# A recurrent LSTM kernel: sigmoid for the output gate, a constant scale of h, and h of the second group in smaller pieces

## What is computed

```
xW = einsum('ntd,dg->ntg', x, Wx) + b
def step(carry, xw_t):
    prev_h, prev_c = carry
    a = xw_t + prev_h @ Wh
    i = sigmoid(a[:, :H]); f = sigmoid(a[:, H:2*H]); o = sigmoid(a[:, 2*H:3*H])
    g = tanh(a[:, 3*H:])
    next_c = f * prev_c + i * g
    next_h = o * tanh(next_c)
    return ((next_h, next_c), next_h)
c0 = zeros_like(h0)
hs = scan(step, (h0, c0), xW by time)
out = x + hs
```

## Time and profile before

| what | value |
|---|---|
| median of 3 runs | 1855.11 us (1855.08 to 1855.83) |
| the profiled execution | 1856.47 us |
| its span, first to last instruction | 1854.4 us |
| granted TensorE clock | 1.000 of full speed |
| busy: PE, DVE, ACT, POOL | 90%, 92%, 55%, 29% |

### The profile page before, as it was taken

How to read it: one execution, slowest core, us unless ns; L and a number is a source line. 1 busy time by engine, 2 the same in 40 slices (tenths; PEclk the granted TensorE clock), 3 DMA queues, 4 the chain that set the end, 5 groups by cost and what they waited for, 6 DMA issues and landing times.

```text
span 1854.4 us, 106048 instructions
## 1 busy us (share of the span) xinstructions
PE 1674.3 (90%) x45116; PEld 1065.3 (57%) x45116; DVE 1713.2 (92%) x9739; ACT 1011.4 (55%) x3985; POOL 539.3 (29%) x1560
## 2 busy tenths in 40 slices
PE   1999999999999999999999999999999999999997
PEld 0555555555555555555555555555555555555555
DVE  8999999999999999999999999999999999999998
ACT  4555555555555555555555555555555555555554
POOL 0222223322332222233223332222232233322222
PEclk9999999999999999999999999999999999999999
DMA  5000000000000000000000000000000000000000
GB/s 210 15 26 21 21 23 23 21 21 26 21 21 26 21 21 21 26 21 21 26 21 21 26 21 21 21 27 21 21 26 21 21 24 24 21 21 27 18 12 14
DMA packets 39067, 49.03 MB, mean 26 GB/s; under 512 B 4416, under 2 KB 36160, under 8 KB 38592
## 3 DMA queue, kind: packets, MB, share of 16 engines
q1 hardware_dynamic: 37152, 37.77, 6.3%
q10 hardware_dynamic: 1440, 4.49, 0.6%
HBM read 25.46 MB, written 16.78 MB: 23 GB/s over the span
## 4 chain that ended last, share of the span: by engine, by line
DVE 70%; PE 19%; ACT 7%; issue 3%; DMA 1%; ACTq 0%; DVEq 0%
DVE turned L510 22%; DVE mailbox L514 13%; PE acc L311 12%; DVE products L523 11%; ACT gates L260 7%; PE acc L317 7%; DVE h_halves L538 5%; DVE h_halves L547 3%; DVE gates L532 3%; DVE x_halves L493 3%; DVE out_ring L575 3%; DVE h_feat L542 3%; DVE x_tops L586 2%; DVE mailbox L528 2%; DMA wh<-in_wh 1%
## 5 line engine op out<-in xcount | busy, mean ns | idle before, releaser
L311 PE MATMUL acc<-wh_low,h_halves 128*32 128x256 f16 x16384 | 719.4, 274 | 135.6 <-DVE h_halves L538 133.8
L317 PE MATMUL acc<-wh_high,h_halves 128*32 128x256 f16 x16384 | 722.3, 275 | 0.0
L303 PE MATMUL x_acc<-wx_high,x_halves 128*32 128x512 f16 x8192 | 621.5, 380 | 1.1 <-ACT x_acc L234 1.1
L311 PEld LDWEIGHTS acc<-wh_low,h_halves 128*32 128x32 f16 x16384 | 390.5, 96 | 395.3 <-DVE h_halves L538 383.8
L260 ACT ACTIVATE gates<-mailbox 128x96 f32<-128x96 f32 x1024 | 257.1, 251 | 634.1 <-DVE mailbox L514 634.1
L510 DVE STREAM_TRANSPOSE turned<-acc 128x256 f32<-128x256 f32 x1024 | 458.9, 448 | 57.2 <-PE acc L317 51.4
L194 POOL TENSOR_SCALAR o_gate<-gates,scales 128x32 f32<-128x32 f32 x1024 | 372.7, 364 | 419.4 <-ACT gates L265 419.4
L186 POOL TENSOR_TENSOR o_preact<-turned 128x32 f32<-128x32 f32 x512 | 163.4, 319 | 892.0 <-DVE turned L510 892.0
L317 PEld LDWEIGHTS acc<-wh_high,h_halves 128*32 128x32 f16 x16384 | 343.6, 96 | 113.8
L303 PE MATMUL x_acc<-wx_low,x_halves 128*32 128x512 f16 x4096 | 399.2, 380 | 0.0
L237 ACT ACTIVATE acc<-x_acc,step_mask 128x512 f32<-128x512 f32 x512 | 334.8, 654 | 4.7 <-PE x_acc L303 4.7
(11 more groups left out here) (67 smaller groups left out, 696.5 us busy)
## 6 DMA issues: line engine op xcount, KB each, us to landing
out<-out_ring SPq DMA_DIRECT2D x128, 128.0 KB, 2.1
x_ring<-in_x SPq DMA_DIRECT2D x120, 128.0 KB, 2.9
wx<-in_wx ACTq DMA_DIRECT2D x4, 512.0 KB, 8.1
wx<-in_wx SPq DMA_DIRECT2D x4, 512.0 KB, 8.1
wh<-in_wh SPq DMA_DIRECT2D x4, 512.0 KB, 16.7
wh<-in_wh ACTq DMA_DIRECT2D x4, 512.0 KB, 17.1
x_ring<-in_x SPq DMA_DIRECT2D x2, 512.0 KB, 16.7
b_rows<-in_b ACTq DMA_DIRECT2D x1, 256.0 KB, 21.4
```

The lines of the kernel that those rows point to most:

```text
L303: last = pe.matmul(x_acc[pair % 2][32 * j:32 * j + 32], x_halves[:, pair % (CHUNK // 2), c, half], w[:, c].rearrange("p (n q) g -> p q n g ...
L311: pe.matmul(acc[par][32 * j:32 * j + 32, n, 0:GL], h_halves[1 - par][:, c, 0:2], w_low["wh"][:, c, n * Q + j], start=False, stop=False, sk ...
L317: last = pe.matmul(acc[par][32 * j:32 * j + 32, n, 0:GL], h_halves[1 - par][:, c, 1:3], w_high["wh"][:, c, n * Q + j], start=False, stop=c ...
```

## The change

The output gate becomes ACT's Sigmoid in place of a tanh and a later (t + 1) / 2, and the scale of h is the constant 2^13 in place of one that follows x. The scale of x is now taken out of the masks by which ACT copies `x_acc` into `acc` (`masks`). So POOL's second instruction (L194) goes, and with it `o_gate`; POOL now adds the output gate's halves of both groups, and DVE's `add_last` goes. `high_of_h` and `full_h` become scalar_tensor_tensor instructions with the constant 2^13, and the output row has the constant 2^-13 in place of a `[128, 1]` operand. In group 1, `full_h` and `low_of_h` are each two instructions on one block (16 elements per partition) in place of one on two blocks; `keep_cell(1)` moves behind them. TensorE waits for the low half of block 2 and of block 3 apart. The wait for the kept cells moves from the end of a step to a place behind `turn(0)` of the next. In the setup, ACT runs a Sigmoid on one element first of all, and DVE makes the scales and inverses with some more small instructions.

The diff, cut to its core. Left out are the declarations of the new tiles, the semaphore counts of the scale steps, and the places where `masks` and `step_inverse` take the place of `inverses`.

```diff
@@ -182,17 +187,10 @@
                 pool.wait_ge(out_free[half], 1)
 
             for t in range(T):
-                pool.wait_ge(turned_ready, NG * t + 1)
-                pool.tensor_tensor(o_preact[0][:], turned[0][:, 6:8, 0, :], turned[0][:, 6:8, 1, :], ALU.add)\
-                    .then_inc(o_preact_ready[0], 1)
-                par = t % 2
-                following = (t + 1) // CHUNK % 2
-                if t + 1 < T and (t + 1) % CHUNK == 0 or t == 0:
-                    pool.wait_ge(x_scale_ready, (t + 1) // CHUNK + 1)
                 for n in range(NG):
-                    pool.wait_ge(o_ready, NG * t + n + 1)
-                    pool.tensor_scalar(o_gate[n][:], gates[par][n][:, 4, :], 1.0, scales[following][:, 1:2], ALU.add, ALU.mult)\
-                        .then_inc(h_parts_ready[n], 1)
+                    pool.wait_ge(turned_ready, NG * t + n + 1)
+                    pool.tensor_tensor(o_preact[n][:], turned[n][:, 6:8, 0, :], turned[n][:, 6:8, 1, :], ALU.add)\
+                        .then_inc(o_preact_ready[n], 1)
 
         @block.scalar
         def _(act):
...
@@ -208,6 +206,8 @@
                 act.activation(w_high[k][:, c, :, 64:GL], w32[k][:, c, :, 64:GL], ACT.Copy, scale=half_scale[:, n:n + 1])\
                     .then_inc(done, 1)
 
+            act.wait_ge(ones_ready, 2)
+            act.activation(one_gate[:], ones[:, 0:1], ACT.Sigmoid)
             act.wait_ge(wx_scale_ready, 1)
             for c in range(C):
                 high_of_w("wx", 0, c, wx_high_done)
...
@@ -227,14 +228,17 @@
             high_of_x(0, 1)
             high_of_w("wh", 1, 2, wh_high_done)
             high_of_w("wh", 1, 3, wh_high_done)
-            act.reg_load(rescale[0], inverses[0][0:1, 3:4])
-            act.reg_load(b_scale[0], scales[0][0:1, 3:4].bitcast(I32))
+            for k in range(2):
+                act.reg_load(first_rescale[k], first_inverse[0:1, k:k + 1].bitcast(I32))
+                act.reg_load(rescale[k], step_inverse[0:1, k:k + 1].bitcast(I32))
+            act.reg_load(b_scale[0], scales[0][0:1, 1:2].bitcast(I32))
 
             def place_bias(pair):
                 act.activation(x_acc[pair % 2][:], b_rows[:], ACT.Copy, scale=b_scale[2 * pair // CHUNK % 2]).then_inc(bias_placed, 1)
 
             def fill(t):
-                act.activation(acc[t % 2][:, :, 0:GL], x_acc[t // 2 % 2][:], ACT.Copy, scale=step_mask[:, t % 2:t % 2 + 1])\
+                mask = masks[t // CHUNK % 2] if t > 0 else step_mask
+                act.activation(acc[t % 2][:, :, 0:GL], x_acc[t // 2 % 2][:], ACT.Copy, scale=mask[:, t % 2:t % 2 + 1])\
                     .then_inc(acc_filled, 1)
 
             act.wait_ge(b_ready, 1)
...
@@ -258,12 +262,12 @@
                 def three_gates(n):
                     act.wait_ge(preact_ready, NG * t + n + 1)
                     act.activation(gates[par][n][:, 1:4, :], preact[n].rearrange("p (g c) b -> p g (c b)", c=2), ACT.Tanh,
-                                   scale=rescale[chunk % 2]).then_inc(gates_ready, 1)
+                                   scale=(rescale if t > 0 else first_rescale)[0]).then_inc(gates_ready, 1)
 
                 def last_gate(n):
                     act.wait_ge(o_preact_ready[n], t + 1)
-                    act.activation(gates[par][n][:, 4, :], o_preact[n][:].rearrange("p c b -> p (c b)"), ACT.Tanh,
-                                   scale=rescale[chunk % 2]).then_inc(o_ready, 1)
+                    act.activation(gates[par][n][:, 4, :], o_preact[n][:].rearrange("p c b -> p (c b)"), ACT.Sigmoid,
+                                   scale=(rescale if t > 0 else first_rescale)[1]).then_inc(h_parts_ready[n], 1)
 
                 def tanh_of_cell(n):
                     act.wait_ge(cell_ready, NG * t + n + 1)
...
@@ -356,12 +359,14 @@
                     pe.wait_ge(h_high_ready, NG * t + 1)
                     recurrent_low(par, 0, (0, 1))
                     recurrent_low(par, 1, (0, 1))
-                    pe.wait_ge(h_ready, NG * t + 1)
+                    pe.wait_ge(h_ready, 3 * t + 1)
                     recurrent_high(par, 0, (0, 1))
                     pe.wait_ge(h_high_ready, NG * t + 2)
                     recurrent_low(par, 0, (2, 3))
-                    pe.wait_ge(h_ready, NG * t + 2)
-                    recurrent_high(par, 0, (2, 3)).then_inc(acc_ready, 1)
+                    pe.wait_ge(h_ready, 3 * t + 2)
+                    recurrent_high(par, 0, (2,))
+                    pe.wait_ge(h_ready, 3 * t + 3)
+                    recurrent_high(par, 0, (3,)).then_inc(acc_ready, 1)
                     recurrent_high(par, 1, (0, 1))
                     recurrent_low(par, 1, (2, 3))
                     recurrent_high(par, 1, (2, 3)).then_inc(acc_ready, 1)
...
@@ -446,9 +451,12 @@
             def scales_of(par):
                 dve.tensor_scalar(scales[par][:], factors[:], acc_scale[:], None, ALU.mult).then_inc(scale_step, 1)
 
-            def inverses_of(par):
-                dve.tensor_scalar(inverses[par][:], scales[par][:].bitcast(I32), -1.0, float(254 << 23), ALU.mult, ALU.add)\
-                    .then_inc(x_scale_ready, 1)
+            def acc_inverse_of():
+                dve.tensor_scalar(acc_inverse[:], acc_scale[:].bitcast(I32), -1.0, float(254 << 23), ALU.mult, ALU.add)\
+                    .then_inc(scale_step, 1)
+
+            def masks_of(par):
+                dve.tensor_scalar(masks[par][:], mask_base[:], acc_inverse[:].bitcast(F32), None, ALU.mult).then_inc(x_scale_ready, 1)
 
             dve.wait_ge(x_sum_ready, 1)
             x_bound_of()
...
@@ -461,28 +469,34 @@
             scale_of(wh_sums, 1, 3)
             dve.tensor_scalar(half_scale[:, 1:2], wh_scale, 0.5, None, ALU.mult).then_inc(wh_scale_ready, 1)
             low_of_w("wx", 0, 1, wx_high_done, wx_low_done)
-            dve.tensor_scalar(top_scale[:], wh_scale, 2.0 ** 13, None, ALU.mult)
+            dve.tensor_scalar(top_scale[:], wh_scale, H_SCALE, None, ALU.mult)
             dve.tensor_scalar(h0_cap[:], wh_scale, h0_scale, None, ALU.mult)
             dve.tensor_copy(factors[:, 0:1], wx_inverse)
-            dve.tensor_scalar(factors[:, 1:2], wh_inverse, 0.5, None, ALU.mult)
-            dve.tensor_copy(factors[:, 2:3], wh_inverse)
-            then(dve.memset(factors[:, 3:4], 1.0))
+            dve.memset(factors[:, 1:2], 1.0)
+            dve.tensor_scalar(step_inverse[:, 0:1], wh_inverse, 1 / H_SCALE, None, ALU.mult)
+            dve.tensor_scalar(step_inverse[:, 1:2], wh_inverse, 2 / H_SCALE, None, ALU.mult)
+            dve.wait_ge(mask_ready, 2 * Q)
+            then(dve.tensor_scalar(mask_base[:], step_mask[:], wh_scale, H_SCALE, ALU.mult, ALU.mult))
             dve.wait_ge(scale_step, 3)
             acc_scale_of()
             dve.wait_ge(scale_step, 4)
             then(dve.tensor_scalar(acc_scale[:], acc_scale[:], h0_cap[:], None, ALU.min))
             scales_of(0)
-            dve.wait_ge(scale_step, 5)
-            inverses_of(0)
+            acc_inverse_of()
+            then(dve.tensor_scalar(h0_scaling[:], acc_scale[:], wh_inverse, None, ALU.mult))
+            dve.wait_ge(scale_step, 6)
+            dve.tensor_copy(first_inverse[:, 0:1], acc_inverse[:].bitcast(F32))
+            then(dve.tensor_scalar(first_inverse[:, 1:2], acc_inverse[:].bitcast(F32), 2.0, None, ALU.mult))
+            masks_of(0)
             low_of_w("wx", 0, 2, wx_high_done, wx_low_done)
             low_of_w("wx", 0, 3, wx_high_done, wx_low_done)
 
             dve.wait_ge(zeroed, 6)
             dve.wait_ge(x_scale_ready, 1)
-            dve.tensor_scalar(h_halves[1][:, :, 1, :], h0_feat[:], scales[0][:, 2:3], None, ALU.mult).then_inc(h_high_ready, NG)
+            dve.tensor_scalar(h_halves[1][:, :, 1, :], h0_feat[:], h0_scaling[:], None, ALU.mult).then_inc(h_high_ready, NG)
             dve.wait_ge(h_high_ready, NG)
-            dve.scalar_tensor_tensor(h_halves[1][:, :, 2, :], h0_feat[:], scales[0][:, 2:3], h_halves[1][:, :, 1, :],
-                                     ALU.mult, ALU.subtract).then_inc(h_ready, NG)
+            dve.scalar_tensor_tensor(h_halves[1][:, :, 2, :], h0_feat[:], h0_scaling[:], h_halves[1][:, :, 1, :],
+                                     ALU.mult, ALU.subtract).then_inc(h_ready, 3)
             dve.wait_ge(b_loaded, 16)
             dve.tensor_scalar(b_rows[:, :, 64:GL], b_rows[:, :, 64:GL], 0.5, None, ALU.mult).then_inc(b_ready, 1)
 
...
@@ -514,10 +527,6 @@
                     dve.tensor_tensor(preact[n], turned[n][:, 0:6, 0, :], turned[n][:, 0:6, 1, :], ALU.add)\
                         .then_inc(preact_ready, 1)
 
-                def add_last(n):
-                    dve.tensor_tensor(o_preact[n][:], turned[n][:, 6:8, 0, :], turned[n][:, 6:8, 1, :], ALU.add)\
-                        .then_inc(o_preact_ready[n], 1)
-
                 def gate_products(n):
                     dve.wait_ge(gates_ready, nth[n])
```

(52 more changed lines are left out.)

24 lines of the change are left out of this document (13 added, 11 removed).

## The result

| kernel | median us | ratio to before, 95% interval |
|---|---|---|
| before | 1855.33 | |
| changed | 1992.56 (1992.50 to 1992.87) | 1.074 (1.0726 to 1.0754) |

A forecast was written before the change was run, and what follows sets the result against it. The prediction took DVE to bound 126 steps without slack, 122 to have 0.06 slack, and PE to bound 264. 13.9 + 6.1 + 0 + setup 0.7 = +20.7 us on 1855.1 gave about 1876, range 1857 to 1891.

The forecast's parts named there:

- What bounds the kernel now: Per step: DVE's way has no slack in 126 steps with L493, 0.06 in 122 with L586; PE bounds 264.
- Group 1 in pieces, and the cheaper output row: End of DVE's step: pieces and longer L538 add 0.165, the output row's constant saves 0.06; what follows starts 0.11 later.
- Tail and setup: End of DVE's step plus more small setup instructions: 13.9 + 6.1 + 0.7, together +20.7 us.
- TensorE's gain of 0.005 and the longer L538: In PE's 264 steps: 0.005 gained from an earlier load, 0.005 lost to the longer L538, net zero.
- W: Theory after the result, not forecast: a second wait in front of add_three(0) starts it 0.07 later, letting POOL start first.
- H: Theory after the result, not forecast: POOL's SBUF-reading add starting just ahead holds DVE's add about 0.085, twice a step.
- POOL's new add, "cost 0": Group 1's output-gate add on POOL in place of L518: done by about 1013.5, before ACT needs it, cost 0.
- R3: Rival, exclusion: L514 of group 1 starts only when POOL's add ends, 0.30 a step, +154, 2030 us; chance 0.05.
- R4: Rival: the Sigmoid brings ACT table loads, four switches a step at 1.28 us, +2620, 4480 us; chance 0.02.

The follow-up runs named there:

- e3: Changed kernel with the kept-cells wait behind add_three(0) and DVE adding group 1's output gate again: 1872.71 us, ratio to before 1.0088.
- e7: e6 with POOL's adds waiting for DVE's add of the same group, no longer for the transpose alone: 1865.57 us, ratio to before 1.0065.
- e10: Kernel before with group 1 in pieces, keep_cell(1) behind them, kept-cells wait in e6's order, output row's operand kept: 1881.90 us, ratio 1.0149.
- e8: e7 with full h and low half of group 1 in one instruction each again: 1853.56 us, ratio to before 1.0000.
- e4: Kernel before with only the kept-cells wait moved between turn(0) and add_three(0): 1937.48 us, ratio to before 1.0437.
- e6: Changed kernel with add_three(0)'s two waits in the other order, transpose first, kept cells second: 1910.54 us, ratio to before 1.0308.
- e2: Changed kernel with DVE adding group 1's output-gate halves again, POOL group 0 alone: 1948.28 us, ratio to before 1.0496.
- e5: Kernel before with only POOL adding group 1's output-gate halves too, DVE's add_last gone: 1899.72 us, ratio to before 1.0249.
- e1: Changed kernel with the kept-cells wait moved behind add_three(0), ahead of turn(1): 1885.53 us, ratio to before 1.0157.
- e9: Changed kernel with POOL's two adds replaced by writes of a constant, same waits and signals: 1905.58 us, ratio to before 1.0277.

## Why the prediction was wrong

- *What bounds the kernel now.* Right: the two kinds of step, no slack behind L493 and 0.06 behind L586. e3, e7 and e10 follow from these numbers.
- *Group 1 in pieces, and the cheaper output row.* Right, a little high. The output row came at 0.47 (0.48 forecast) and cost 0.14 (0.14); the steps became 0.09 and 0.02 longer where 0.11 and 0.05 were forecast. The first `turn(0)` comes at 51.85 where it came at 51.18: 0.67 for the setup (0.7). Tail and setup together were put at 20.7 us; e3 has 16 and e7 12, and what lies between these two is open.
- *TensorE's gain of 0.005 and the longer L538.* The gain is there, 0.006 between e7 and e8. The loss isn't: L547 in the changed kernel lasts 0.18 like L538 in the earlier trace rows.
- *The moved wait* had no term in the sum. The text costs L518, L194, L538, L542, L575, the pieces and the setup, and passes over the wait. It failed by omission: the wait stands between two instructions of the chain, and any change there had to be costed at both ends. A bound was at hand only in part. No row of before shows two waits ahead of an instruction that is due at once: its trace has two waits ahead of `add_three(1)` at step 6 of 31 chunks, but `gate_products(0)` stands between the transpose and the add there, and the add starts as in the other steps. W costs 0.07 directly and 0.085 through H, 0.155 a step, 80 us (e4, e6).
- *POOL's new add, "cost 0".* Wrong by 0.085 a step, 45 us (e2, e5). R3 had the mechanism and the point from which it decides, POOL ahead by any margin. Its price, 0.30, was more than three times too high, and its chance, 0.05, too low. The evidence against it was a row that couldn't bear it: L528, which starts 0.12 after L194 and isn't held. The distance isn't the reason. At 0.13 behind POOL's add the same instruction is held in e1 (0.25 in place of 0.19), and behind L194 it isn't held at 0.05 either, in 31 steps of before such as this:

```profile
1006.16 0.32 POOL L194 TENSOR_SCALAR o_gate<-gates,scales 128x32 f32<-128x32 f32 x1 [0.48 <-ACT gates L265]
1006.21 0.19 DVE L528 SCALAR_TENSOR_TENSOR mailbox<-products 128x32 f32<-128x32 f32 x1
```

It is the other POOL instruction: L194 is a tensor_scalar with one tensor from SBUF, the new add has two. Which of the two differences counts, the kind or the second tensor, no run shows. The same rows held a sign that was not read: L194 took 0.39 where it started 0.04 behind L514, and 0.32 in the steps where it started 0.12 behind it, so it was held in its turn, as POOL's adds of 0.32 and 0.25 in e5 show.
- *The sum, put right:* 512 x 0.155 = 79.4 for the wait and group 0, 512 x 0.085 = 43.5 for group 1, and e7's or e3's 12 to 16 for tail and setup: 135 to 139 us, measured 137.

The Trainium skill, SBUF — State Buffer, "Who interferes with whom", says that a VectorE instruction with two SBUF inputs contends with a GpSimd instruction that reads SBUF, not with one that only writes it. e5 and e9 agree on both halves (0.35 against 0.27); L528 at its usual 0.19, 0.05 behind the start of L194, does not. That page of the Trainium skill says under "SBUF: two separate sides" that the one that starts first has the shared ports for its whole instruction and the other is blocked; here DVE's add was held for 0.085 while POOL's lasted 0.25, so the measurement decides against that size.

ScalarE: Activation LUTs of the Trainium skill, "Table sets: the hidden batching unit", lists tanh in sigmoid's set. The trace agrees: the Sigmoid, ACT's L269, has 226 ns and no idle time before it in the page's group, among tanh instructions, where a load would be 1283 ns; the trace's only table load is in the setup, as before. R4 falls by these rows.

## What to carry to other kernels

Where two engines are released by the same instruction and both read SBUF, look at the order in which they start, not only at whether they overlap: 0.03 us decides which of them pays, and the one off the chain should be given a later release. A second wait is free if the wait that ends last is carried by the instruction itself; write that wait first, and look in the chain for the sequencer's name. And a row clears a rival only for the pair of instructions and the distance with which it was taken.
